# Attention re-planned: the tiles on the diagonal move from the front to the end of each block of queries

## What is computed

```python
def _L0_attn_ref(x, Wq, Wk, Wv, Wo, bo):
    q = (x @ Wq).reshape(b, n, NUM_KV_GROUPS, GROUP_SIZE, HEAD_DIM)
    k = (x @ Wk).reshape(b, n, NUM_KV_GROUPS, HEAD_DIM)
    v = (x @ Wv).reshape(b, n, NUM_KV_GROUPS, HEAD_DIM)
    scores = jnp.einsum('bqgsd,bkgd->bgsqk', q, k) * scale
    causal = jnp.arange(n)[:, None] < jnp.arange(n)[None, :]
    scores = jnp.where(causal, -jnp.inf, scores)
    attn = jax.nn.softmax(scores, axis=-1)
    ctx = jnp.einsum('bgsqk,bkgd->bqgsd', attn, v)
    return ctx.reshape(b, n, D_OUT) @ Wo + bo
```

## Time and profile before

| | |
|---|---|
| Median of the runs | 2770.99 us |
| Lowest and highest of the 3 runs | 2770.24 and 2773.05 us |
| The profiled execution's own time | 2771.73 us |
| Its span, first to last instruction | 2770.0 us |
| Attention within it | from 224 us to about 1340 us |
| PE busy in attention | 1065.7 of 1116 us |

### The profile page before, as it was taken

The page is one execution under the profiler, slowest core; times in us unless marked ns, Lnnn a source line. Parts: engine busy times, 40 slices in busy tenths (PEclk is TensorE's granted clock), DMA queues, the critical chain, the costliest instruction groups (busy, mean ns, idle before and its releaser), DMA issues. The chain is left out here.

```text
span 2770.0 us, 40600 instructions
## 1 busy us (share of the span) xinstructions
PE 2589.9 (93%) x14178; PEld 1808.6 (65%) x14178; DVE 1713.5 (62%) x3567; ACT 1436.7 (52%) x2768; POOL 982.6 (35%) x601
## 2 busy tenths in 40 slices
PE   6997999999999999999696999999999999699998
PEld 5784545454555545553475788888788888588886
DVE  3225777777777777783496544446554454467776
ACT  1221546555555556565487555556554554345453
POOL 6000455655565656566693000000000000245554
PEclk9996999999999999999897999999999999899999
DMA  6444012121111111110597323225432332675453
GB/s 216 163 163 115 22 34 60 44 60 41 49 47 43 49 49 47 43 33 9 172 347 253 112 85 115 100 91 177 135 111 80 114 103 88 217 254 162 124 164 103
DMA packets 204212, 304.34 MB, mean 110 GB/s; under 512 B 39376, under 2 KB 85488, under 8 KB 199792
## 3 DMA queue, kind: packets, MB, share of 16 engines
q1 hardware_dynamic: 200768, 294.72, 34.0%
q0 software_dynamic: 1600, 5.24, 0.5%
q10 hardware_dynamic: 1648, 1.88, 0.2%
HBM read 184.83 MB, written 116.42 MB: 109 GB/s over the span
## 5 line engine op out<-in xcount | busy, mean ns | idle before, releaser
L782 ACT ACTIVATE p_probs<-p_ps_s 128x512 f32<-128x512 f32 (+3 forms) x1280 | 598.3, 537 | 420.6 <-PE p_ps_s L715 413.4
L809 DVE TENSOR_REDUCE p_parts<-p_ps_m 128x1 f32<-128x512 f32 x768 | 477.4, 681 | 126.7 <-PE p_ps_m L703 126.0
L703 PE MATMUL p_ps_m<-p_k_m,p_q 96*128 96x512 f32 (+3 forms) x1280 | 480.2, 405 | 25.2 <-DMA p_q<-q_t 11.7
L715 PE MATMUL p_ps_s<-p_q,p_k_e 98*128 98x512 f32 (+3 forms) x1280 | 461.5, 386 | 29.1 <-DMA p_q<-p_rows 21.8
L672 POOL TENSOR_TENSOR p_added<-p_added,p_probs 128x2048 f32<-128x2048 f32 x88 | 403.2, 4582 | 32.5 <-ACT p_probs L782 23.9
L703 PEld LDWEIGHTS p_ps_m<-p_k_m,p_q 96*128 96x128 f32 x1280 | 247.8, 198 | 234.9 <-DVE p_parts L809 93.8
L715 PEld LDWEIGHTS p_ps_s<-p_q,p_k_e 98*128 98x128 f32 x1280 | 243.3, 195 | 161.9 <-ACT p_probs L782 70.3
L1671 POOL MEMSET p_power<- 128x1 f32 x1 | 0.1, 98 | 891.0 <-POOLq L1849 891.0
L733 PE MATMUL p_ps_c<-p_probs,p_v 128*32 128x512 f32 (+3 forms) x2560 | 306.8, 552 | 1.1 <-ACT p_probs L782 0.7
L813 DVE CUSTOM_DVE_ANT_0 p_masked<-p_ps_m,p_mask 128x384 f32<-128x384 f32 (+3 forms) x512 | 226.2, 487 | 122.5 <-PE p_ps_m L703 120.2
L73 PE MATMUL p_ps_l<-p_xT_hi,p_mu_hi 128*128 128x512 f32 x512 | 207.7, 406 | 16.4 <-DVE p_xT_lo L1500 11.7
(11 more groups left out here) (181 smaller groups left out, 4678.7 us busy)
## 6 DMA issues: line engine op xcount, KB each, us to landing
logits_t<-p_logit SPq DMA_DIRECT2D x32, 1024.0 KB, 5.0
p_lg<-logits_t SPq DMA_DIRECT2D x128, 256.0 KB, 3.7
p_q<-q_t SPq DMA_DIRECT2D x96, 256.0 KB, 4.7
p_w_raw<-L_ffn_W_dram SPq DMA_DIRECT2D x64, 256.0 KB, 5.4
p_so<-slot_out SPq DMA_DIRECT2D x32, 512.0 KB, 6.6
p_x<-L_attn_x_dram SPq DMA_DIRECT2D x8, 1024.0 KB, 6.3
q_t<-p_f_hi SPq DMA_DIRECT2D x32, 256.0 KB, 2.5
q_t<-p_f_lo SPq DMA_DIRECT2D x32, 256.0 KB, 2.6
```

What stands on the lines that cost most here:

```text
L703: pe.matmul(ps_m[:, u % M_BANKS, 0:w], q[0:QROWS, qb, h, bass.ts(t, P)], k_m[:, c * BLK:c * BLK + w], start=True, stop=True).then_inc(s_un ...
L715: pe.matmul(ps_s[:, u % ST_BANKS, q0:BLK], k_e[:, bass.ts(kt, P)], q[:, qb, h, q0:BLK], start=True, stop=True).then_inc(s_score, 1)
L782: act.activation(probs[s % RING][:, h, q0:BLK], ps_s[:, u % ST_BANKS, q0:BLK], ACT.Exp).then_inc(s_exp, 1)
L809: dve.tensor_reduce(to, bank, AX.X, ALU.max).then_inc(s_taken, 1)
```

## The change

It has four parts.

1. `block_order` takes the full tiles in order and the four tiles on the diagonal last.
2. `ADDED` lists one tile more for each of the three larger blocks: 20 of the 24 full tiles of an iteration where 17 were listed. POOL makes 17 `add` instructions in an iteration, 136 in all, where it made 14 and 112.
3. DVE's `maximum_rows` computes the lower half of the split with a `tensor_reduce` over pairs, where it used a `tensor_tensor` of two SBUF operands; for this it writes the maximum once with each sign.
4. The planner gets other costs (2300 ns becomes 5400 ns from the last maximum's rows to their being in place, entering and leaving a group cost more) and other rules: a group is begun only when ACT and DVE each have 1.5 us of work queued (`fed`), or when the ring is full or nothing else can run, and goes on to at most 1.7 us (`longest`).

```diff
 def block_order(qb):
 
-    return list(range(4 * qb, 4 * qb + 4)) + list(range(4 * qb))
+    return list(range(4 * qb + 4))
 
...
-ADDED = [[], [0, 1, 2], [0, 1, 2, 4, 5, 6], [0, 1, 3, 4, 6, 7, 9, 10]]
+ADDED = [[], [0, 1, 2, 3], [0, 1, 2, 3, 4, 5, 7], [0, 1, 3, 4, 5, 6, 8, 9, 11]]
...
-    HOP, LAND, ENTER, LEAVE = 90, 200, 86, 114
+    HOP, LAND, ENTER, LEAVE, AGAIN = 90, 200, 140, 114, 105
+    SHORT = {P: 110, 2 * P: 123, 3 * P: 177, 4 * P: 233}
...
         if u + 1 in M_END:
-            self.dve += 850
-            self.rows[n] = self.dve + 2300
+            self.dve += 950
+            self.rows[n] = self.dve + ROWS
...
+ROWS = 5400
...
+        length = 830 if owed is not None else context_time(c) if c < s else 0
+        now = [x for x in ((k.act + lead, scores, 0), (k.dve, maximum, 1)) if x[1] <= k.pe + near]
+        if packed <= k.pe + 60 and (k.run + length <= longest or not now if k.packed else
+                                    min(k.act, k.dve) - k.pe >= fed or s - c >= RING - press or not now and min(scores, maximum) > k.pe + idle):
             what = 2
...
                 dve.wait_ge(s_taken, M_END[n])
-                dve.tensor_reduce(neg[:, :], parts[n % 2][:, :, 0:qb + 1], AX.X, ALU.max, negate=True).then_inc(s_neg, 1)
-                dve.tensor_reduce(split[:, 0:16], parts[n % 2][:, :, 0:qb + 1], AX.X, ALU.max, negate=True).then_inc(s_neg, 1)
-                dve.wait_ge(s_neg, 3 * n + 2)
-                dve.tensor_tensor(split[:, 16:32], neg[:, :], split[:, 0:16], ALU.subtract).then_inc(s_neg, 1)
-                dve.wait_ge(s_neg, 3 * n + 3)
+                part = parts[n % 2][:, :, 0:qb + 1]
+                dve.tensor_reduce(pairs[:, :, 0], part, AX.X, ALU.max, negate=True).then_inc(s_neg, 1)
+                dve.tensor_reduce(pairs[:, :, 1].bitcast(F32R), part, AX.X, ALU.max).then_inc(s_neg, 1)
+                dve.tensor_reduce(split[:, 0:16], part, AX.X, ALU.max, negate=True).then_inc(s_neg, 1)
+                dve.wait_ge(s_neg, 4 * n + 3)
+                with nc.allow_low_precision(reason="the rounded low half of a sum of two"):
+                    dve.tensor_reduce(split[:, 16:32], pairs[:, :, :], AX.X, ALU.add).then_inc(s_neg, 1)
+                dve.wait_ge(s_neg, 4 * n + 4)
```

More of the change, by code:

```diff
@@ L344, in diagonals_to @@
 def diagonals_to(s):
-    return 4 * STEPS[s][0] + min(s - FIRST[STEPS[s][0]], 3) + 1
+    n = STEPS[s][0]
+    return 4 * n + s - (END[n] - 4) + 1
 def is_added(s):
@@ L352, in is_added, with first_direct @@
     return kt in ADDED[BLOCKS[n][1]]
+def first_direct(n):
+    return min(s for s in range(FIRST[n], END[n]) if not is_added(s))
 def adds_to(s):
@@ L368 @@
 class Clock:
-    HOP, LAND, ENTER, LEAVE = 90, 200, 86, 114
+    HOP, LAND, ENTER, LEAVE, AGAIN = 90, 200, 140, 114, 105
+    SHORT = {P: 110, 2 * P: 123, 3 * P: 177, 4 * P: 233}
     def __init__(self):
         self.pe = self.act = self.dve = self.pool = 0.0
-        self.packed = False
+        self.packed, self.again, self.run = False, False, 0.0
         self.maxed, self.scored, self.expd, self.chosen, self.summed = {}, {}, {}, {}, {}
@@ L378, in __init__ @@
         self.work, self.moves = [], []
+        self.groups, self.stall = 0, {"m": 0, "s": 0, "c": 0}
     def matmul(self, ready, columns):
-        self.pe = max(self.pe, ready) + max(64, 0.452 * columns + 3) + (self.LEAVE if self.packed else 0)
-        self.packed = False
+        if self.packed:
+            self.pe += self.LEAVE
+        extra = self.AGAIN if self.again else 0
+        self.again, self.packed = self.packed, False
+        self.wait = max(0, ready - self.pe)
+        self.pe = max(self.pe, ready) + self.SHORT[columns] + extra
         return self.pe + self.LAND
     def packed_products(self, ready, columns, count):
-        self.pe = max(self.pe, ready) + count * 1.6 * columns + (0 if self.packed else self.ENTER + self.LEAVE)
+        first = 0 if self.packed else self.ENTER
+        self.run = 0.0 if first else self.run
+        self.groups += first > 0
+        self.stall["c"] += max(0, ready - self.pe)
+        self.run += count * 1.62 * columns
+        self.pe = max(self.pe, ready) + count * 1.62 * columns + first
         self.packed = True
@@ L411, in maximum @@
         width = unit_width(u)
-        self.dve = max(self.dve, self.matmul(self.maximum_ready(u), width) + self.HOP) + 85 + 1.045 * width + (85 if c == BLOCKS[n][1] else 0)
+        scored = self.matmul(self.maximum_ready(u), width)
+        self.stall["m"] += self.wait
+        self.dve = max(self.dve, scored + self.HOP) + 1.042 * width + (79 if c == BLOCKS[n][1] else 65)
         self.maxed[u] = self.dve
@@ L428, in scores @@
         self.scored[u] = self.matmul(self.scores_ready(s, h), columns)
+        self.stall["s"] += self.wait
         begin = max(self.act, self.scored[u] + self.HOP)
@@ L446, in scores @@
         if qb == QB - 1 and it + 1 < ITERS and s - FIRST[n] in (3, 7, 11, 15):
-            c = ((s - FIRST[n]) // 4 + QB - 1) % QB
+            c = (s - FIRST[n]) // 4
             self.moves.append((self.scored[u], "keys", (it + 1, c, s + 1)))
@@ L473, in inverse @@
     def inverse(self, n):
-        self.flipped[n] = max(self.dve, self.pe + self.LAND + self.HOP) + 710
-        self.dve = self.flipped[n] + 1000
-        self.pool = max(self.pool, self.dve + self.HOP) + 1300
+        self.flipped[n] = max(self.dve, self.pe + self.LAND + self.HOP) + 740
+        self.dve = self.flipped[n] + 940
+        self.pool = max(self.pool, self.dve + self.HOP) + 1290
         self.work += [("inverse", n, None), ("normalise", n, None)]
@@ L481, with context_time, plan @@
 INF = 1e18
+ROWS = 5400
+def context_time(s):
+    return (1 if is_added(s) else 2) * 1.62 * (BLK - first_query(s))
 @lru_cache(maxsize=None)
-def plan():
+def plan(fed=1500, lead=300, longest=1700, idle=50, press=0, near=0):
     k, u, s, h, c, owed = Clock(), 0, 0, 0, 0, None
@@ L492, in plan @@
         packed = k.sums_ready(owed) if owed is not None else k.context_ready(c) if c < s else INF
-        now = [x for x in ((k.act + 300, scores, 0), (k.dve, maximum, 1)) if x[1] <= k.pe + 40]
-        if packed <= k.pe and (not now or s - c >= RING - 2):
+        length = 830 if owed is not None else context_time(c) if c < s else 0
+        now = [x for x in ((k.act + lead, scores, 0), (k.dve, maximum, 1)) if x[1] <= k.pe + near]
+        if packed <= k.pe + 60 and (k.run + length <= longest or not now if k.packed else
+                                    min(k.act, k.dve) - k.pe >= fed or s - c >= RING - press or not now and min(scores, maximum) > k.pe + idle):
             what = 2
@@ L498, in plan @@
         else:
-            what = min((scores, 0), (maximum, 1), (packed, 2))[1]
+            what = min((scores, 0), (maximum, 1), (packed if packed > k.pe + 60 or min(scores, maximum) > k.pe + idle else INF, 2))[1]
         if what == 0:
@@ L541, in attention @@
         masked = [al.sbuf(f"p2_masked{r}", [P, BLK]) for r in range(4)]
-        neg = al.sbuf("p2_neg", [P, 16])
+        pairs = al.sbuf("p2_pairs", [P, 16, 2])
         split = al.sbuf("p2_split", [P, 32], F32R)
@@ L738, in context @@
                         mm = pe.matmul(ps_d[part, 0, q0:BLK], ones[:, :], probs[s % RING][:, h, q0:BLK],
-                                       start=s == FIRST[n], stop=last and not ADDS[qb])
+                                       start=s == first_direct(n), stop=last and not ADDS[qb])
                 mm.then_inc(s_ctx, 1)
```

2 lines of the change are left out of this document (1 added, 1 removed).

## The result

The changed kernel takes 2689.24 us (median; 2687.57 to 2689.88) against 2771.01 us. The ratio is 0.9703, with a 95% interval from 0.9686 to 0.9720: 3.0% less time. The forecast was 2687 us with a range from 2670 to 2714. The total is met within 3 us, but not all of its terms are, as the experiments show.

What follows compares the result with a forecast made beforehand. PE was taken to bound attention through its work, groups and one wait for rows. Savings of 20.4 + 33.6 + 36.4 - 7 + 1 = 84.4 us from 2771.73 gave a forecast of 2687 us, range 2670 to 2714.

Steps and rivals of the forecast that it cites:

- The bound: Attention: PE is full, busy 129 of 132 us an iteration, its time being work, groups and one wait for maximum rows.
- Part 1: Attention: three more tiles an iteration leave PE's sum matmuls for POOL, 24 sets x 0.85 us = 20.4 us saved.
- Part 2: PE in attention: 341 groups of packed matmuls become 245, 96 x 0.35 us = 33.6 us saved.
- third rival: Attention: longer groups run DVE and ACT dry, 0.2 us in half the groups, 25 us lost, 2712 us; chance 0.12.
- Part 3: Attention iterations: PE's wait for the maximum rows goes, with the half clock behind it; 17.7 + 18.7 = 36.4 us saved.
- Part 4: Attention: context of the first diagonal tile waits for its select behind POOL's adds; 0.9 us an iteration, 7 us lost.
- The last block: Last block of attention: POOL's adds count at the end; 52 us instead of 55.0, adding 1 us to the saving.
- The start: First 146 us of attention, bound by DVE and the first blocks' rows: left as it is, 8 us to either side.
- The first: Attention: PE still stands 2 us or more an iteration, for a select or the rows; clock falls, 2717 us; chance 0.13.
- The second: Attention: POOL keeps its 53 us idle and becomes the bound; an iteration takes 146 us, kernel 2883 us; chance 0.03.

Runs made afterwards that it cites:

- e3: The changed kernel with the earlier list of added tiles (17 of 24 in an iteration instead of 20), diagonal still last: 2710.9 us, ratio 0.9779.
- e5: The changed kernel with the planner's old rule for beginning and ending a group, new costs kept, 337 groups instead of 245: 2710.3 us, ratio 0.9770.
- e6: The kernel before with only the split by reductions and the maximum rows planned at 950 and 5400 ns instead of 850 and 2300: 2725.0 us, ratio 0.9825.
- e4b: The changed kernel with 17 added tiles and the diagonal first in each block as before, 269 groups: 2719.0 us, ratio 0.9814.
- e7: The kernel before with the split by reductions alone, plan and order as they were: 2759.4 us, ratio 0.9952.
- e1: The changed kernel with the split by a tensor_tensor of two SBUF operands put back: 2695.9 us, ratio 0.9722.
- e8: The changed kernel with all 24 full tiles of an iteration added on POOL, 168 adds for 136: 2745.2 us, ratio 0.9900.

## Why the prediction was right, point by point

**The bound** was read rightly. PE's products and groups at the prices of the earlier trace rows still make 96% of an iteration, and only what shortened PE's own queue, or a wait in it, moved the time.

**Part 1, the sums (20.4 us).** e3 gives 20 to 22 us for these and 25 groups, for which I would have said 29. Its iterations have 3.7 us of short waits where those of the changed kernel have 4.7, 8 us in eight, and that is the difference. So the products are rightly priced, and a part of the saving comes back as short waits.

**Part 2, the groups (33.6 us): the mechanism right, the size wrong.** The price of 0.35 us is confirmed in the trace. But e5 gives 21 us for 92 groups where the step says 32. From e6 to e4b, which has 70 groups fewer, 6 us are gained where it says 24.5 (there the planner's other costs change as well). I had weighed this as the third rival, at 25 us, and put it at 0.12. It happened, beside the other gains: an iteration of the changed kernel has 3.1 us more of short waits than one of e6, 25 us in eight.

**Part 3, the rows (36.4 us): right for the two halves together, wrong in how they share it.** The wait is gone, the slack is there, the reductions take 0.2 us each, and the clock stays at 1.00. e6 measures 48 us, because the wait had struck in the start too (10.3 us less there), where I counted nothing. I had traced DVE's delay rightly to the add that runs beside it, but took its 1.8 us for a part of the rows' way. In the old order the quick split alone leaves the wait for the rows at 17.7 us, and its 13 us come from elsewhere (e7); in the new order the slow split brings no wait for the rows back (e1). So it is the planned figure, and the work that the plan puts into the gap, that takes the wait away. The figure without the split was not run in the old order. What I had not looked at is the loads that stand ahead of the rows in SP's queue.

**Part 4, POOL's queue (7 us).** In the iterations it cost nothing that can be seen. At the second largest block of the third iteration the adds and the select ran like this:

```profile
558.25 4.59 POOL L700 TENSOR_TENSOR p_added<-p_probs 128x2048 f32<-128x2048 f32 x1 [4.34 <-ACT p_probs L810]
...
573.51 14.06 POOL L700 TENSOR_TENSOR p_added<-p_added,p_probs 128x2048 f32<-128x2048 f32 x3
587.51 1.81 POOL L685 TENSOR_SCALAR_AFFINE_SELECT p_probs<-p_probs 128x512 f32<-128x512 f32 x3
```

The first select is done at about 588.1. With the 0.6 us for the exponentials ahead of its first add POOL has needed the 30.5 us of the reckoning. PE comes to that tile's context at 588.87, 0.8 us later, where the reckoning had it 0.4 us too early. So the size for POOL was right and PE is the slower by some 1.2 us; its short waits, 4.7 us an iteration, are the likely reason.

**The last block (52 us expected, 55.3 measured)** was reasoned rightly, POOL's adds being last. They begin 8.4 us into the block (1200.1 to 1208.5), as reckoned. What I left out is the 2.0 us between the first add and the other seven (1213.07 to 1215.10, a normalise and a wait for ACT), and from the first select's end it takes 6.9 us (1248.53 to 1255.45) and not 6.

**The start (left as it was, 8 us to either side): it gained 22.** This is the step that failed. The prediction calls the start bound by DVE and by the rows of the first blocks, and then counts nothing for it. Only the share of parts 1 and 2 that falls there is in the sum, 3 sets and 7 groups by the traces, 5 us. PE's waits in it before, from 224 to 420 us and without the first load, were 19.0 us:

```profile
PE p_ps_m L703 <- DVE p_parts L813: 6.1, 7, 1.8
PE p_ps_s L715 <- DMA p_q<-p_rows: 4.1, 3, 1.7
PE p_ps_m L703 <- DVE p_parts L809: 3.6, 4, 2.0
PE p_ps_s L715 <- ACT p_probs L782: 3.5, 1, 3.5
PE p_ps_s L715 <- issue: 1.7, 1, 1.7
```

Now they are the 3.4 us for DVE shown above. The steps from before to changed are 10.3 us for the rows (e6, 8.5 us of waits left), 2.1 back for the new rule and costs (e4b), 3.7 for the order (e3, 6.2 left) and 10.2 for the three tiles. Why the last step is so large is open.

So the total is right by luck, by two misses that cancel: the iterations and the last block gave 62 us where the sum had 79, and the start gave 22 where it had 5. An iteration takes 122.5 us, outside the 119 to 120.5 that I had named.

**The rivals.** The first did not happen: no dip of the clock is left in the iterations. The second, POOL as the bound, did not happen either, but e8 shows that it needs no POOL near 100%: with 4 tiles more POOL is busy 86% and already sets the pace, where the changed kernel has it at 76%.

## What to carry to other kernels

When an order is made ahead by a model, first compare its delays with the trace: one figure, the 2.3 us for a transfer that takes 5 or more, together with a two-operand instruction behind GpSimd's add, cost 48 of the 82 us, and mending the instruction alone gave 13. A quicker step pays only as far as the next queue lets it, here SP's. Price a kind of work from the spacing of starts, but do not book the whole saving where several engines are fed by turns: of the saving in groups a third to three quarters came back as gaps too short to show as idle. And when work moves to an in-order engine, look at the place where nothing else hides it, here the last block, and give that place less.
